# A two-layer decoder on one core: the order of the shared experts' products, the filling products before the routed experts, and the place of the row gathers

## What is computed

```
logits = flat @ gate_w;  scores = softmax(logits) + gate_b;  topi = top 2 of 16 experts
per expert: the 320 tokens of largest weight among those that chose it
    y = (silu(xs @ ew1) * (xs @ ew3)) @ ew2 * weight      # 128 -> 256 -> 128
out = scatter-add of the y + mean of two shared experts (same form, all tokens)
x = x + out
x = x + attention1(layernorm(x))    # 16 heads of 8, relative positions, 512 x 512 scores
```

## Time and profile before

| | |
|---|---|
| median of three runs | 1465.93 us |
| profiled execution, its own time | 1466.06 us |
| its span | 1464.3 us |
| granted TensorE clock over the span | 0.935 of full |
| busy share TensorE / VectorE / ScalarE / GpSimd | 89 / 67 / 49 / 41 % |
| the chain that ended last | 69 % TensorE, 16 % VectorE, 6 % issue, 4 % ScalarE, 2 % GpSimd |

### The profile page before, as it was taken

How to read it: one execution, slowest core, us unless ns; L and a number is a source line. 1 busy time by engine, 2 the same in 40 slices (tenths; PEclk the granted TensorE clock), 3 DMA queues, 4 the chain that set the end, 5 groups by cost and what they waited for, 6 DMA issues and landing times.

```text
span 1464.3 us, 29550 instructions
## 1 busy us (share of the span) xinstructions
PE 1299.7 (89%) x10946; PEld 943.6 (64%) x10946; DVE 981.9 (67%) x2399; ACT 712.9 (49%) x1472; POOL 603.3 (41%) x712
## 2 busy tenths in 40 slices
PE   7999999999999699715299988879999999989998
PEld 5666767777677366412158656657777776767887
DVE  5988877777776678686013356457786889866554
ACT  4666666667676266300003325345666666634221
POOL 4555556555565100101701337665575565501110
PEclk9999999999999799856699989789999999999999
DMA  6140000000000200000013221412021121000000
GB/s 186 34 130 16 1 1 2 1 2 1 1 1 1 65 2 2 1 0 3 16 32 87 61 47 43 118 19 52 23 54 36 39 51 26 13 1 1 1 0 29
DMA packets 76999, 43.88 MB, mean 30 GB/s; under 512 B 26089, under 2 KB 71738, under 8 KB 76870
## 3 DMA queue, kind: packets, MB, share of 16 engines
q1 hardware_dynamic: 72342, 38.56, 9.9%
q10 hardware_dynamic: 2480, 2.29, 0.5%
q0 software_dynamic: 2048, 1.27, 0.4%
HBM read 21.89 MB, written 10.49 MB: 22 GB/s over the span
## 4 chain that ended last, share of the span: by engine, by line
PE 69%; DVE 16%; issue 6%; ACT 4%; POOL 2%; SPq 1%; DMA 1%; another core or an unknown queue 0%; DVEq 0%; POOLq 0%; ACTq 0%
PE psum L1237 7%; PE psum L1625 7%; PE psum L1222 7%; PE psum L1212 6%; PE psum L1734 6%; PE psum L1745 4%; PE psum L1637 4%; PE psum L1609 3%; PE psum L1616 3%; PE psum L1447 2%; PE psum L1188 2%; PE psum L1246 2%; PE psum L1149 2%; PE psum L1194 1%; PE psum L1457 1%
## 5 line engine op out<-in xcount | busy, mean ns | idle before, releaser
L606 POOL TENSOR_TENSOR arena<-arena,rden 128x512 f32<-128x512 f32 x256 | 260.9, 1042 | 209.7 <-DVE rden L1895 209.6
L871 ACT ACTIVATE arena<-psum,negmax 128x512 f32<-128x512 f32 x256 | 175.0, 692 | 151.0 <-DVE negmax L1886 131.7
L1886 DVE TENSOR_REDUCE negmax<-psum 128x1 f32<-128x512 f32 x256 | 168.0, 681 | 55.5 <-PE psum L1212 54.9
L2400 DVE TENSOR_REDUCE negmax<-psum 128x1 f32<-128x512 f32 x256 | 164.8, 684 | 57.3 <-PE psum L1616 50.7
L1222 PEld LDWEIGHTS psum<-cst,arena 128*128 128x128 f32 x1024 | 113.1, 141 | 44.7 <-issue 44.3
L1222 PE MATMUL psum<-cst,arena 128*128 128x128 f32 x1024 | 138.1, 276 | 3.2 <-DVE arena L1881 0.8
L1609 PE MATMUL psum<-a_kstack,a_qblk 96*128 96x512 f32 x256 | 99.5, 471 | 10.2 <-POOL wqkv L701 8.2
L1212 PE MATMUL psum<-a_qk 64*128 64x512 f32 x768 | 106.0, 407 | 2.5 <-DVE a_qk L1904 2.5
L1734 PE MATMUL psum<-f_h,f_w 128*128 128x512 f32 x384 | 101.3, 414 | 7.2 <-DVE arena L2498 7.1
L1066 ACT ACTIVATE kT<-psum,negmax 128x512 f32<-128x512 f32 x64 | 44.0, 687 | 109.9 <-PE psum L1625 75.5
L1212 PEld LDWEIGHTS psum<-a_qk 64*128 64x128 f32 x768 | 67.4, 184 | 38.9 <-issue 24.2
(11 more groups left out here) (338 smaller groups left out, 2831.6 us busy)
## 6 DMA issues: line engine op xcount, KB each, us to landing
w<-in_ew SPq DMA_DIRECT2D x2, 2048.0 KB, 8.3
a_kstack<-a_khi SPq DMA_DIRECT2D x64, 64.0 KB, 2.0
xs_rows<-f SPq DMA_DIRECT2D x3, 1024.0 KB, 5.3
arena<-xs_rows SPq DMA_DIRECT2D x8, 384.0 KB, 4.0
ys_rows<-wqkv SPq DMA_DIRECT2D x8, 384.0 KB, 2.6
a_kstack<-a_klo SPq DMA_DIRECT2D x32, 64.0 KB, 2.0
a_kstack<-a_khi SPq DMA_DIRECT2D x64, 32.0 KB, 1.9
a_qstack<-a_qhi SPq DMA_DIRECT2D x120, 16.0 KB
```

The costliest lines, as they stand in the source:

```text
L606: pool.tensor_tensor(a0_p[u % 4], a0_p[u % 4], rden[:, u:u + 1].broadcast_to([P, SEQ]), ALU.mult).then_inc(a0_norm, 1)
L871: act.activation(a0_p[u % 4], bank[u % 4][:, :], ACT.Exp, bias=negmax[:, u:u + 1], accum_out=den[:, u:u + 1]).then_inc(a0_exp, 1)
L1886: dve.tensor_reduce(negmax[:, u:u + 1], bank[u % 4][:, :], AX.X, ALU.max, negate=True).then_inc(a0_max, 1)
L2400: dve.tensor_reduce(negmax[:, n % 8:n % 8 + 1], bank[n % 4][:, :], AX.X, ALU.max, negate=True).then_inc(a1_max, 1)
```

## The change

The change has four parts.

1. TensorE's shared experts: all eight steps of the first layer of two batches, then both second layers, whole, with bank 0 for the even and bank 7 for the odd batch. The wait for the other batch's addition goes for batches 0 and 1, and is for batch c - 2's addition in batches 2 and 3. VectorE's additions move behind its eight products; those of batches 2 and 3 both come after the 12 steps of pre_norm.
2. The 26 filling products before the routed experts become five, and they stand behind the wait for r_pad. The memset that gives r_pad moves on GpSimd from before the routing's end into the scatter, behind the 28th of its 32 DMAs.
3. The two filling products before the last second layer go.
4. The 24 gathers of batches 1 to 3 are issued one at a time, at seven places of GpSimd's turn: seven in turn 0, four in turn 1, six in turn 2, three each in turns 3 and 4, one in turn 5. Place 1 is behind stage_q(it, 1), 2 behind stage_v, 3 behind low_k, 4 behind the early guest, 5 behind stage_q(it + 1, 0), 6 behind the late guest and 7 behind output_bias(0).

```diff
--- before.py
+++ after.py
@@ GpSimd: the memset of hs' padding, and the scatter @@
             for g in range(2):
                 pool.memset(gathered[g], 0.0).then_inc(gath_zero, 1)
-            pool.memset(hs[:, :, :, CAP:], 0.0).then_inc(r_pad, 1)
...
             for t in range(NT):
+                if t == NT - 2:
+                    pool.memset(hs[:, :, :, CAP:], 0.0).then_inc(r_pad, 1)
                 for c in range(2):
                     pool.indirect_dma_start(xs_rows, ...).then_inc(scattered, 16)
@@ GpSimd: the gathers @@
-            def gather(first, last):
-                for t in range(first, last):
-                    for c in range(2):
-                        pool.indirect_dma_start(gathered[c][:, t, :], None, ys_rows, ...).then_inc(got[t // QT], 16)
-
-            gather(0, QT)
+            def gather(t, c):
+                pool.indirect_dma_start(gathered[c][:, t, :], None, ys_rows, ...).then_inc(got[t // QT], 16)
+
+            for t in range(QT):
+                for c in range(2):
+                    gather(t, c)
...
+            GATHER_AT = ((1, 2, 3, 4, 5, 6, 7), (1, 3, 5, 6), (1, 2, 3, 4, 5, 6), (2, 4, 6), (2, 4, 6), (2,))
+            rest = [(t, c) for t in range(QT, NT) for c in range(2)]
+
+            def gather_one(it, slot):
+                if it < len(GATHER_AT) and slot in GATHER_AT[it]:
+                    gather(*rest[sum(len(slots) for slots in GATHER_AT[:it]) + GATHER_AT[it].index(slot)])
...
             for it in range(NT):
                 stage_q(it, 1)
+                gather_one(it, 1)
                 stage_v(it)
+                gather_one(it, 2)
                 if it < NT - 1:
                     low_k(it + 1)
-                if it == 0:
-                    gather(QT, QT + QT // 2)
+                gather_one(it, 3)
                 guest_norm(it, False)
+                gather_one(it, 4)
                 if it < NT - 1:
                     stage_q(it + 1, 0)
+                gather_one(it, 5)
                 if it % QT == QT - 2 and it < NT - QT:
                     low_q(it // QT + 1)
                 guest_norm(it, True)
-                if it < B - 1:
-                    gather((it + 1) * QT + (0 if it else QT // 2), (it + 2) * QT)
+                gather_one(it, 6)
                 if it == 0:
                     output_bias(0)
+                gather_one(it, 7)
@@ TensorE: the shared experts @@
-            def shared_down(c, first):
-                if first:
-                    pe.wait_ge(sh_hid, 4 * c + 4)
-                    if c:
-                        pe.wait_ge(sh_x, c)
-                for t in range(2 * (1 - first), 2 * (1 - first) + 2):
+            def shared_down(c):
+                pe.wait_ge(sh_hid, 4 * c + 4)
+                if c >= 2:
+                    pe.wait_ge(sh_x, c - 1)
+                for t in range(QT):
                     for k in range(4):
-                        mm = pe.matmul(bank[0][:, t * P:(t + 1) * P], ...)
-                if not first:
-                    mm.then_inc(sh_y, 1)
+                        mm = pe.matmul(bank[7 * (c % 2)][:, t * P:(t + 1) * P], ...)
+                mm.then_inc(sh_y, 1)
...
             def shared_chunks(first, last):
                 for u in range(4 * first, 4 * last):
                     shared_up(u)
-                    if u >= 4 * first + 4 and u % 4 in (1, 2):
-                        shared_down(u // 4 - 1, u % 4 == 1)
-                if first:
-                    keep_busy(bank[1], 2)
-                for half in (True, False):
-                    shared_down(last - 1, half)
+                for c in range(first, last):
+                    shared_down(c)
 
             pe.wait_ge(pre_act, 3)
             shared_chunks(0, 2)
-            keep_busy(bank[2], 26)
             pe.wait_ge(r_pad, 1)
+            keep_busy(bank[2], 5)
             routed_turn(0, True)
@@ VectorE: adding the shared experts to X @@
             for u in range(8):
                 shared_hid(u)
-                if u == 7:
-                    shared_add(0)
-            shared_add(1)
+            for c in range(2):
+                shared_add(c)
             routed_turn(0, True)
...
             for u in range(8, 16):
                 shared_hid(u)
-            shared_add(2)
...
             for step in range(12):
                 pre_norm(0, step)
-            shared_add(3)
+            for c in range(2, B):
+                shared_add(c)

```

More of the change, by code:

```diff
@@ L643, in _ @@
             pool.wait_ge(gath_zero, 2)
-            def gather(first, last):
-                for t in range(first, last):
-                    for c in range(2):
-                        pool.indirect_dma_start(gathered[c][:, t, :], None, ys_rows, bass.IndirectOffsetOnAxis(ap=g_row[:, c, t:t + 1], axis=0),
-                                                bounds_check=ROWS - 1, oob_is_err=False).then_inc(got[t // QT], 16)
-            gather(0, QT)
+            def gather(t, c):
+                pool.indirect_dma_start(gathered[c][:, t, :], None, ys_rows, bass.IndirectOffsetOnAxis(ap=g_row[:, c, t:t + 1], axis=0),
+                                        bounds_check=ROWS - 1, oob_is_err=False).then_inc(got[t // QT], 16)
+            for t in range(QT):
+                for c in range(2):
+                    gather(t, c)
             pool.wait_ge(r_staged, E0)
@@ L754, in guest_norm @@
                     batch_norm(b, scale_count("f1", b), ln_ready)
+            GATHER_AT = ((1, 2, 3, 4, 5, 6, 7), (1, 3, 5, 6), (1, 2, 3, 4, 5, 6), (2, 4, 6), (2, 4, 6), (2,))
+            assert sum(len(slots) for slots in GATHER_AT) == (B - 1) * QT * 2
+            rest = [(t, c) for t in range(QT, NT) for c in range(2)]
+            def gather_one(it, slot):
+                if it < len(GATHER_AT) and slot in GATHER_AT[it]:
+                    gather(*rest[sum(len(slots) for slots in GATHER_AT[:it]) + GATHER_AT[it].index(slot)])
             low_k(0)
@@ L1418, in shared_up @@
                 mm.then_inc(sh_h, 1)
-            def shared_down(c, first):
-                if first:
-                    pe.wait_ge(sh_hid, 4 * c + 4)
-                    if c:
-                        pe.wait_ge(sh_x, c)
-                for t in range(2 * (1 - first), 2 * (1 - first) + 2):
+            def shared_down(c):
[3 more added lines that the diff above has]
+                for t in range(QT):
                     for k in range(4):
-                        mm = pe.matmul(bank[0][:, t * P:(t + 1) * P], sh_hidden[c % 2][:, k, t * P:(t + 1) * P],
+                        mm = pe.matmul(bank[7 * (c % 2)][:, t * P:(t + 1) * P], sh_hidden[c % 2][:, k, t * P:(t + 1) * P],
                                        w2[:, E0 + k // 2, k % 2, :], start=(k == 0), stop=(k == 3))
-                if not first:
-                    mm.then_inc(sh_y, 1)
+                mm.then_inc(sh_y, 1)
             def routed_t(e, k, first):
@@ L2177, in shared_add @@
                 xc = X[:, c * QT:(c + 1) * QT, :]
-                dve.scalar_tensor_tensor(xc, bank[0][:, :].rearrange("p (t d) -> p t d", d=D), 1.0 / NSH, xc, ALU.mult, ALU.add).then_inc(sh_x, 1)
+                dve.scalar_tensor_tensor(xc, bank[7 * (c % 2)][:, :].rearrange("p (t d) -> p t d", d=D), 1.0 / NSH, xc, ALU.mult, ALU.add).then_inc(sh_x, 1)
             dve.wait_ge(g_chain, 200)
```

## The result

The kernel after took 1418.04 us (median of 4 runs, 1416.96 to 1420.2), the kernel before 1466.1 on the same chip (4 runs, 1461.05 to 1468.77). The ratio is 0.9682, 95% interval 0.9661 to 0.9703: 48 us less, where 43.1 had been forecast (1423.0). The profiled execution of after has a span of 1415.1 us.

A forecast was written before the change was run, and what follows sets the result against it. Bounds: filling products delaying the routed experts, and GpSimd's back-to-back scatters and gathers delaying TensorE's updates. 25.6 + 2.0 + 1.5 - 2.6 + 12.9 + 7.6 - 3.9 = 43.1; 1466.1 - 43.1 = 1423.0 us, range 1410 to 1443.

The forecast's parts named there:

- Start of the routed experts: TensorE's transposes of the routed experts start at 735.6 instead of 762.80; 25.6 us gained after a 1.6 cold start.
- Second half: Second shared part of the experts: VectorE begins pre_norm sooner, no longer behind shared_add(2); 2.0 us gained.
- Turn 0: Layer 1's attention, turn 0: of VectorE's 7.19 us wait around four gathers, 1.5 us gained, bounds 0 and 4.7.
- Turn 1: Layer 1's attention, turn 1: two gathers delay GpSimd's addition and batch_norm(1) by 1.28 us each; 2.6 us lost.
- Turn 2: Layer 1's attention, turn 2: the run of eight gathers goes, 14.4 us less 1.5 for late updates; 12.9 gained.
- Turn 3: Layer 1's attention, turn 3: the 10.23 us gather run before stage_q(3, 1) goes, two gathers stay; 7.6 us gained.
- the prediction's last sentence: Prediction wrong if TensorE still dribbles in turn 2, or new waits of 2 us or more stand beside single gathers.
- Single gathers: Eleven lone gathers in turns 1 to 5, charged 0.35 us each for late updates; 3.9 us lost, bounds 0 and 14.
- Rival 1: Shared experts' silu 7 stays stuck to the scatter's end, transposes at 745.4; gain there 17.4, total 1431.2 us; chance 0.15.
- Rival 3: Each lone gather in the turns holds updates, at 3 us each; net 12.6 us slower, 1478.7 us; chance 0.05.
- rival 4: Something else holds the routed experts' start to about 760 and the turns give nothing net; no change; chance 0.03.
- Rival 2: TensorE's stalls aren't the gathers' doing but instruction supply or SyncE's copies; gain 32.6, 1433.5 us; chance 0.12.

The follow-up runs named there:

- the third chip: A chip where the kernel before took 1420.75 us and the unchanged kernel after 1413.7, ratio 0.9941; the 32 scatters did not hold TensorE there.
- the added run: Kernel after plus 2, 4 and 8 unbroken indexed DMAs from GpSimd at the ends of turns 5, 9 and 13: 1425.3 us.
- the spaced one: Kernel before plus eight unbroken indexed gathers in turn 9 and eight separated by memsets in turn 13: 1480.99 us, ratio 1.0113.
- the run with skipped rows: Kernel after plus 2, 4 and 8 indexed DMAs in turns 5, 9 and 13, with bounds_check=0 so nearly nothing moves: 1429.31 us.

## Why the prediction was right, and where it was not

The mechanism held and the sum was 6 us short of the 49.1 of the traces. Of these, 3.9 each are turn 0 and the single gathers and 1.3 turn 2; the start of the experts, 2.5 too high, hid part of them. By its own steps, with gains of the traces:

- **Start of the routed experts**: 25.6 forecast, 23.1 measured. The step "silu 7 should run near 705" held and was even cautious (701.13). The step after it failed: "batch 1's second layer near 706 to 713". I had taken the held thing to be TensorE's updates alone, as the late silu of before suggested; TensorE's own issue is held as well, in a place where before had nothing to issue and so could not show it. The second layer ended at 731.8, the fills came behind it and took 6.3 us. With no fills the transposes start at 735.57. That this is the forecast's 735.6 is partly chance: the held layer sets it, in an execution 1.2 us late, and the landing, which I took at 4.4 us from the asking, is 3.4 on the third chip. The five fills cost 4.1 us, or 5.3 counted from the first scatter, and save the cold start, which I had charged with 1.6 and which measured 2.3.
- **Second half**: 2.0 forecast, 25.3 - 23.1 = 2.1 measured. What ends last there is the landing of the gathers.
- **Turn 0**: 1.5, measured 5.4, just above my bound of 4.7. (It has seven gathers now where it had eight, not "still seven".) The 7.19 us wait is gone. With the gathers spread alone the turn gave only 0.6, with fills alone 2.8. In all of these the kernels' granted clock differs in this turn (stretches of 8 or 9 us at 0.85 in before, at 0.78 and 0.81 with the gathers alone, 1.00 from 853 to 879 in after), so part of it may be the clock. What decides it was not settled.
- **Turn 1**: -2.6, measured -2.9. VectorE's wait went from 1.36 to 2.74, as forecast, and moving the two gathers took the loss away.
- **Turn 2**: 12.9 (14.4 less 1.5), measured 14.2. The four gathers of places 1 to 4, which start 1.3 to 2.4 us apart (900.65 to 906.65), cost nothing that the trace shows. Closer ones would have: an unbroken run of four cost 1.4 us in a later turn, and in the version with turn 1's gathers moved, where two stand together beside turn 2's value products, 1.1 us went.
- **Turn 3**: 7.6, measured 7.2. This was GpSimd's own time and needed no held engine. "The keys remain the last wait there" held: the wait grew from 1.49 to 4.63 us. By the prediction's last sentence a new wait of 2 us or more in turns 1 to 5 was to count against it; this is one such, but the engine waits for the keys by name, and no product is held.
- **Single gathers**: -3.9, measured 0 for the four in turns 4 and 5: from turn 4 on the two traces keep the same distance to 0.1 us. The seven in turns 1 to 3 can't be told from the rest of their turns, which came out within 1.3 us of the forecast without them. The term was mis-sized; a lone gather costs only what it delays on GpSimd.

Rival 1 (the silu stays stuck) is what happens without the new order (744.70 against its 745.4). Rival 3 (each lone gather holds updates) is refuted by the same 0 and by the total, and rival 4 (no change) by the start of the experts and by the turns. Rival 2 (the stalls aren't the gathers' doing) is refuted three times: by the gathers alone, by the added run and by the spaced one. The rule of the Trainium skill behind it, "SBUF — State Buffer", section "Who interferes with whom", isn't contradicted in what it speaks of, memory ports, since the run with skipped rows moves next to nothing and holds TensorE all the same. But whoever concludes from it that GpSimd's DMAs can't slow TensorE is wrong by 9.2 us for a run of eight.

The range's lower end has two slips: turn 0's bound of 4.7 is 3.2 above the 1.5 taken, not 1.4, and the start's bound of 28 is 2.4 above 25.6, not 1.6. With these the favourable sum is 1410.2 and not 1412.8, still inside the range.

What I left out altogether is that the effect may not be on every chip. Had the change been timed on the third one alone, the forecast would have missed by 9 us and the gain would have been 0.6%.

## What to carry to other kernels

Don't let GpSimd issue indexed DMAs in an unbroken run while TensorE has many short products to issue. Two alone, or one each 2.4 us, cost 0.3 us at most, four cost 1.4 us, and eight cost 8 to 9 us in the later turns and 10 to 14 in turn 2. Beside the 32 scatters TensorE ran on for 18 us and then issued 19 pieces in 25 us. The eight gathers of batch 0, beside which TensorE had only some 37 pieces to issue, cost nothing in after. If a run can't be broken, put nothing beside it that the path needs, and no filling work behind it. Place a single one by GpSimd's own queue: ahead of a step that someone waits for it costs its 1.3 us, elsewhere nothing. Look at "issue" gaps of a microsecond in an engine's timeline, and at long waits called "remote", and lay them against what GpSimd does.

## What the runs showed of the hardware

- A run of indexed DMAs from GpSimd (0.97 to 1.0 us each, 0.30 apart) can hold TensorE's issue to one to four pieces per DMA, beginning at the third or fourth DMA of a run of eight in the turns and after some 18 us of the 32 scatters, and VectorE or ScalarE then waited 27.5 to 31.8 us for an update beside the scatters. With rows skipped the hold is the same.
- Not every such run does. Beside the eight gathers of batch 0 TensorE issued about 37 pieces in 10.2 us, half of them 128x512, without a gap that "issue" ends, in before and in after; beside the runs in the turns it issued 29 to 51 short pieces in the 3 to 4 us before its first gap. Whether it is this pace that decides was not tested. In before one silu was late there (843.09 for products done at 841.41), in after none.
- Beside the scatters TensorE and the updates were held on three of the four chips of the experiments, in each of their traces; on one they were not, at the same pace of the DMAs.
- Right behind the filling pieces the granted clock was 1.00 in after, and the experts' first group of 16 pieces took 4.88 us. On the third chip, where TensorE idled 3.07 us between, it was 0.77 and the group took 6.50, little less than without fills (6.86). TensorE had also idled 15.68 us before the filling pieces there, so which of the two idle times did it is not shown. Stretches of after, and of after on that chip:

```profile
740.00:745.50 5.50, 5.18 (x22) 3.33 (x21) 2.32 (x5) 1.31 (x3) 0.61 (x1) 1.00 0.26 72
```

```profile
734.00:741.50 7.50, 7.18 (x22) 4.67 (x23) 2.36 (x5) 1.31 (x3) 0.61 (x1) 0.77 0.26 70
```
